# Throwaway transposes of the identity in the waits of TensorE, in a macaron block on one Trainium2 core

## What is computed

```python
x = L0_attn_x                                    # (8, 512, 128)
x = x + 0.5 * ffn(layernorm(x), weight, bias, delta_w, delta_act)
x = x + attn(layernorm(x), wq, wk, wv and their biases)
x = x + 0.5 * ffn(layernorm(x), weight, bias, delta_w, delta_act)

# ffn: x_q and w_q are rounded to MXFP4 in blocks of 32 with a tweaked power-of-two scale
ffn  = einsum('bsd,od->bso', x_q, w_q) + bias
# attn: q and k get rotary positions, 16 heads of 8 numbers
attn = softmax(q @ k.T / sqrt(8)) @ v
```

## Time and profile before

| | |
|---|---|
| time, median of 3 runs | 534.62 us (534.57 to 535.41) |
| profiled execution | 534.99 us, of which the span is 533.2 us |
| TensorE matmuls busy | 455.7 us, 85% of the span |
| VectorE busy | 437.7 us, 82% |
| ScalarE busy | 383.2 us, 72% |
| GpSimd busy | 234.0 us, 44% |
| mean granted TensorE clock | 0.957 |

### The profile page before, as it was taken

The page is one execution under the profiler, slowest core; times in us unless marked ns, Lnnn a source line. Parts: engine busy times, 40 slices in busy tenths (PEclk is TensorE's granted clock), DMA queues, the critical chain, the costliest instruction groups (busy, mean ns, idle before and its releaser), DMA issues.

```text
span 533.2 us, 8358 instructions
## 1 busy us (share of the span) xinstructions
PE 455.7 (85%) x2564; PEld 153.0 (29%) x2564; DVE 437.7 (82%) x996; ACT 383.2 (72%) x750; POOL 234.0 (44%) x340
## 2 busy tenths in 40 slices
PE   2252999999989998999999998999899989998941
PEld 1121232333223232333233323323232323222211
DVE  6863999898899889997999799988997889897125
ACT  7854158678778887787868887787787877777730
POOL 8330065336644465545553656356543624112200
PEclk9985599999999999999999999999999999999995
DMA  5015311321122213221222112221222132100000
GB/s 163 23 49 139 89 52 51 90 92 50 51 90 91 68 36 94 73 75 33 78 77 87 59 51 90 91 71 50 91 85 67 30 91 91 50 2 2 22 0 20
DMA packets 27960, 34.86 MB, mean 65 GB/s; under 512 B 6278, under 2 KB 21260, under 8 KB 27916
## 3 DMA queue, kind: packets, MB, share of 16 engines
q1 hardware_dynamic: 26068, 33.35, 20.6%
q10 hardware_dynamic: 1848, 0.98, 0.7%
HBM read 21.34 MB, written 8.39 MB: 56 GB/s over the span
## 4 chain that ended last, share of the span: by engine, by line
PE 57%; DVE 24%; issue 7%; ACT 5%; POOL 4%; DMA 2%; SPq 0%; POOLq 0%; ACTq 0%; DVEq 0%
PE ot L1138 17%; PE sc L1125 16%; DVE negmax L915 13%; PE st L1114 12%; ACT probs L668 3%; PE misc L1063 2%; PE misc L1080 2%; PE misc L1103 2%; DVE stats_f L784 1%; PE misc L1088 1%; PE misc L1096 1%; PE misc L1058 1%; DMA feat_q<-parts_q 1%; PE misc L1071 1%; PE misc L1047 1%
## 5 line engine op out<-in xcount | busy, mean ns | idle before, releaser
L915 DVE TENSOR_REDUCE negmax<-sc 128x1 f32<-128x512 f32 x512 | 329.6, 682 | 49.2 <-PE sc L1125 48.9
L668 ACT ACTIVATE probs<-st 128x512 f32<-128x512 f32 x512 | 272.7, 599 | 76.9 <-PE st L1114 74.8
L1125 PE MATMUL sc<-feat_k,feat_q 96*128 96x512 bf16 x512 | 186.7, 393 | 18.2 <-DVE negmax L915 10.3
L1114 PE MATMUL st<-feat_q,feat_k 99*128 99x512 bf16 x512 | 155.9, 380 | 8.0 <-ACT probs L668 7.8
L1138 PE MATMUL ot<-probs,vfeat 128*32 128x512 f32 x1024 | 136.2, 604 | 1.1 <-ACT probs L668 1.0
L1125 PEld LDWEIGHTS sc<-feat_k,feat_q 96*128 96x128 bf16 x512 | 49.7, 97 | 169.0 <-DVE negmax L915 101.7
L1114 PEld LDWEIGHTS st<-feat_q,feat_k 99*128 99x128 bf16 x512 | 49.4, 98 | 78.0 <-ACT probs L668 48.9
L466 POOL TENSOR_SCALAR maxparts<-negmax 128x16 bf16<-128x16 f32 x32 | 8.5, 266 | 73.4 <-DVE negmax L915 73.4
L450 POOL TENSOR_TENSOR xs_f<-xc_f,magic_f 128x512 f32<-128x512 f32 x14 | 17.8, 1270 | 36.9 <-DVE magic_f L878 36.9
L425 POOL TENSOR_TENSOR rstd_f<-ve_f,nhalf 128x4 f32<-128x4 f32 x16 | 16.6, 1035 | 37.0 <-DVE nm_f L796 31.7
L1138 PEld LDWEIGHTS ot<-probs,vfeat 128*32 128x32 f32 x1024 | 20.2, 108 | 37.5 <-ACT probs L668 20.0
(11 more groups left out here) (134 smaller groups left out, 461.3 us busy)
## 6 DMA issues: line engine op xcount, KB each, us to landing
feat_q<-parts_q SPq DMA_DIRECT2D x96, 96.0 KB
feat_k<-parts_k SPq DMA_DIRECT2D x90, 96.0 KB
qkswap<-qkpre SPq DMA_DIRECT2D x32, 128.0 KB, 2.0
parts_q<-qkparts_q SPq DMA_DIRECT2D x24, 128.0 KB, 2.3
parts_k<-qkparts_k SPq DMA_DIRECT2D x24, 128.0 KB, 2.3
xres<-in_L_attn_x_dram SPq DMA_DIRECT2D x8, 256.0 KB, 4.9
out_dram<-xres SPq DMA_DIRECT2D x8, 256.0 KB, 2.5
feat_k<-parts_k ACTq DMA_DIRECT2D x6, 96.0 KB
```

What stands on the lines that cost most here:

```text
L668: nc.scalar.activation(probs[:, s % US, j * S:(j + 1) * S], st[:, bank(2 * s + j), :], ACT.Exp, scale=SCALE).then_inc(exp_done, 1)
L915: nc.vector.tensor_reduce(negmax[:, g, j:j + 1], sc[:, bank(16 * g + j), :], AX.X, ALU.max, negate=True).then_inc(sc_maxed, 1)
L1114: nc.tensor.matmul(st[:, bank(2 * s + j), :], feat["k"][par][0:MROWS, h, kb * P:(kb + 1) * P], feat["q"][par][0:MROWS, h, :], start=True, ...
L1125: nc.tensor.matmul(sc[:, bank(16 * g + j), :], feat["q"][par][0:SROWS, h, t * P:(t + 1) * P], feat["k"][par][0:SROWS, h, :], start=True, s ...
```

## The change

A helper `keep_warm(n, bank)` issues n f32 transposes of the identity into a PSUM bank that nobody reads at the time. It waits for nothing and signals nothing. It is called in five places of TensorE's queue: 8 transposes ahead of `turn_xn` of batch 0, 12 behind `project_v` of batch 0, 16 behind `mul_w` of `f1` of batch 1, 24 ahead of `turn_xq` of `f2` of batch 7, and 4 between that `turn_xq` and its `mul_w`. Nothing is removed or moved.

```diff
+            def keep_warm(n, bank):
+
+                for i in range(n):
+                    nc.tensor.transpose(bank[:, i % T * P:(i % T + 1) * P], ident[:, :], ident[:, :])
+
             def turn_xn(b):
...
                     for n, first in (("f2", -1), ("f1", 2)):
                         for nb, _ in turns(b, par, s, n, "turn", first):
+                            if (n, nb) == ("f2", B - 1):
+                                keep_warm(24, sc[:, 0, :])
                             turn_xq(n, nb)
                         for nb, _ in turns(b, par, s, n, "mul", first):
+                            if (n, nb) == ("f2", B - 1):
+                                keep_warm(4, sc[:, 0, :])
                             mul_w(n, nb)
+                            if (n, nb) == ("f1", 1):
+                                keep_warm(16, ot)
                     for nb, _ in turns(b, par, s, "pj", "turn", 2):
+                        if nb == 0:
+                            keep_warm(8, sc[:, 2, :])
                         turn_xn(nb)
...
                     for nb, _ in turns(b, par, s, "pj", "v", 2):
                         project_v(nb)
+                        if nb == 0:
+                            keep_warm(12, ot)
```

## The result

The changed kernel takes 535.86 us, median of 20 runs (534.56 to 536.95), against 534.69 of 20 runs of the kernel before (533.36 to 535.41). The ratio is 1.0022, 95% interval 1.0014 to 1.003: 1.2 us slower (0.7 to 1.6). I had forecast no measurable change, 534.7. The profiled execution takes 536.0 us, its span is 534.2.

The account below looks back on a forecast made before the run. TensorE's low clock was taken to count in only three places: first projection, first scores to second projection, and the end. Terms 0 + 0 + 0 + 0 + 0.1 us gave 534.7 us, range 532.6 to 535.6; chance of same 0.72.

Parts of the forecast that it names:

- Cost nothing: Prologue: the 8, 12 and 16 transposes fit inside TensorE's waits, ending at 23.0, 36.7 and 48.5 us; 0 us added.
- the 0.03 for a slower case that I don't see: Anywhere in the kernel: chance 0.03 left for an unnamed slower cause, out of 0.05 left over.
- the slower rival that I named: Last wait, before `mul_w`: the four transposes do not fit; without overlap 1.84 us late, 536.5; chance 0.05.
- The first projection: Batch 0, 26.18 us: clock still low after the 8 transposes, gain nothing; rival with clock up 533.0, chance 0.06.
- the 3.7 us of work that I held to be too little: TensorE's work from 19.30 to 23.0 us, against 5.8 and about 6 before rises seen; no rise expected.
- The first scores: At 52.60 us: clock low again after 4.1 us of waiting behind the 16, gain nothing; rival clock up, chance 0.10.
- My price for a clock held to 68 us, 1.7: First scores to second projection: rival saves 0.22 on the first tile plus VectorE's idle 0.19 + 1.27; 532.9, chance 0.10.
- The 24: Ahead of the last `turn_xq`: run from 514.8 to 518.4 at most, 8.0 us or more left; cost and gain nothing.
- the 3.1 and 3.6 I had: Delays in us from the last matmul to the clock's fall, two falls seen at 37.2 and 518.4 us.
- The 4: Between last `turn_xq` and `mul_w`: 0.88 us of transposes in a 0.77 us wait, so 0.1 us longer.
- The price at the end: Last feed-forward: rival with clock up saves 0.8 on matmuls and some 0.2 on transposes, 1.0 us; 533.6, chance 0.02.

Follow-up runs that it names:

- e4: The changed kernel with 4 transposes in place of 16 behind the first feed-forward's matmuls of batch 1; ratio to the kernel before 1.0019 (1.0009 to 1.0029).
- e10: The changed kernel with the 16 transposes held back until the write of the k parts has landed; ratio to the kernel before 0.9991 (0.9982 to 1.0).
- e1: The kernel before with 72 instructions of satisfied waits at the prologue's three places, no transposes, nothing at the end; ratio 1.0 (0.9991 to 1.0009).

## Why the prediction was wrong

- **The step that failed** is the sentence "Cost nothing" of the three places in the prologue. I costed 36 transposes by the time TensorE takes for them, 8.0 us in waits of 4.9, 3.6 and 7.7, and that was right: none delayed any work of TensorE. What I left out is that they are 72 instructions, and that here the load of a block of instructions held up a write of data for 0.6 us or more. They brought the next load from 66 us to 44, into the one write on which the first scores wait. The term I had at 0 is 1.2 us (0.7 to 1.6) in the first measurement and 0.9 (0.4 to 1.3) in the second. With the load moved away and all 64 transposes kept it is 0 again, within 0.5. Only the 0.03 for a slower case that I don't see covers this; the slower rival that I named was another one.
- The Trainium skill (Runtime: NRT & Kernel Launch, section "Instruction fetch mechanics") states that instructions come in blocks of 16 KiB, 256 instructions each, over a DMA queue of the sequencer's own, and that the cost is mostly hidden. The size of a block agrees with the trace: 0.33 MB in 20 packets; how many instructions it holds no run here shows. From TensorE the cost is hidden here too: the 16 transposes run on through the load. From the kernel it is not: a load took 0.9 to 1.7 us of one DMA engine, and in five runs of five with the load at 44 us the write beside it was 0.6 to 1.45 late.
- **The first projection**: right in the changed kernel's trace, and that was luck. Transposes 1.11 and q matmuls at 28 us as before, the clock low. But with the same work up to there the clock was up at 26.18 in the traces of e4 and e10, until 26.3 and 26.7: it had risen behind the 3.7 us of work that I held to be too little, and in e10 the chain was 0.4 us earlier for it. In the changed kernel it rose by 31.6 instead of 33.8, which made the v matmuls faster and a little of k's, and nothing on the chain waits for those.
- **The first scores**: right, and close. The clock rose with the end of the 16 and fell 3.6 us later, at 51.9. That is 0.7 us before 52.60, where the scores started in the kernel before. My price for a clock held to 68 us, 1.7, is not contradicted: the version that holds it there and at the end is 2.6 us faster (1.9 to 3.3), and the end alone 1.3 (0.7 to 1.9), which leaves 1.3 for the scores.
- **The 24**: right. They ended at 518.4, the clock fell at 523.0, and the work came at 527.35 at low clock. The fall was 4.6 us behind them, longer than the 3.1 and 3.6 I had. The Trainium skill's example (TensorE: Matmul & The Clock Gate, section "Seeing it yourself") has 5.2. The fall behind the 16, where 5.2 would have changed the time, came after 3.6.
- **The 4**: 0.02 where I had 0.1; they start at 527.75, and nearly all of their time lies beside ScalarE's copy, for which the bias matmul waits anyway.
- **The price at the end**: I had 1.0 us for a clock held there; the run that does it measures 1.3 (0.7 to 1.9), and its timeline shows 1.03.

## What to carry to other kernels

Filler work costs instructions as well as engine time: look in the profile for where the instruction queue's packets fall before and after, and whether a transfer that something waits for is under way then; here 118 satisfied waits earlier in the queue, or holding the filler back until that transfer had landed, moved the packet out of its way. Filler without a wait runs at the beginning of a gap: the 24 transposes did nothing for work 9 us behind them, while 100 that reached to 0.65 us before the end of the same wait won 1.3 us. Where tiles are sparse, filler ahead of them was not enough, and two transposes between them held the clock at 1.00.

## What the runs showed that I had not expected

- One 16 KB load of instructions keeps one DMA engine busy for 0.9 to 1.7 us; a write spread over all sixteen then ends up to 1.45 us later (2.30 to 3.75).
- The clock's fall is not a fixed time behind the last matmul: 3.1, 3.6, 3.6 and 4.6 us in the kernel before and the changed one, and only 0.2 us at 38.3 in the changed one, behind four short transposes in a long wait. Nor is the rise fixed by the work before it: by 31.6 us in the changed kernel, before 26.2 in e4 and e10 with the same work up to there. With one score tile per 0.60 us it fell in the middle of the work, at 55.1 us.
- 72 instructions ahead of the first scores brought the next load at 44 us when they were transposes and at 46 when they were waits. Counted in the traces, 164 of TensorE's instructions had started when it came in the changed kernel and 202 in e1. So TensorE seems to take transposes in ahead of their run and waits not; no run tests this by itself.
